# Moving the MAX8 over the candidate sums ahead of the first one-hots in a product-key expert kernel

## The reference, cut to what matters

```
xn  = batchnorm(x) * gamma + beta
sim = einsum(q(xn), keys)                  # per token, 8 heads, 2 sides, 32 keys
s, i = top_k(sim, 8)                       # (sx, ix) and (sy, iy)
all_scores = sx[..., :, None] + sy[..., None, :]
scores, pk = top_k(all_scores, 8)          # of 64 sums per head
idx = (ix * 32 + iy)[pk]                   # one of 1024 experts
o   = gelu(x . key_in[idx]) * softmax(scores)
out = layernorm(x + sum over heads and k of o * key_out[idx])
```

## Time and profile before

| | |
|---|---|
| time, median of 3 runs | 588.12 us (588.06 to 588.79) |
| the profiled execution's own time | 586.68 us |
| its span in the trace | 584.9 us |
| DVE busy | 490.1 us, 84% of the span |
| TensorE matmul, ACT, POOL busy | 308.8, 263.6 and 288.7 us |

### The profile page before, as it was taken

How to read it: one execution, slowest core, us unless ns; L and a number is a source line. 1 busy time by engine, 2 the same in 40 slices (tenths; PEclk the granted TensorE clock), 3 DMA queues, 4 the chain that set the end, 5 groups by cost and what they waited for, 6 DMA issues and landing times.

```text
span 584.9 us, 14423 instructions
## 1 busy us (share of the span) xinstructions
PE 308.8 (53%) x5105; PEld 198.8 (34%) x5105; DVE 490.1 (84%) x2777; ACT 263.6 (45%) x416; POOL 288.7 (49%) x307
## 2 busy tenths in 40 slices
PE   5687575124142818272836465446545563456845
PEld 3233462013122316132722252226223521442544
DVE  2557896899899989899898989998989898984834
ACT  4877523314233642574166325812671455225721
POOL 1143411361623689278917881867198639840000
PEclk9898765665555758695769595958586877597988
DMA  8800000000023003200410050005000500140051
GB/s 232 239 0 2 0 2 1 1 0 3 2 56 92 1 3 90 68 10 2 119 47 2 2 145 21 1 2 145 21 1 13 135 20 1 30 117 1 16 150 36
DMA packets 49848, 26.69 MB, mean 46 GB/s; under 512 B 3056, under 2 KB 49008, under 8 KB 49776
## 3 DMA queue, kind: packets, MB, share of 16 engines
q1 hardware_dynamic: 49200, 25.70, 16.9%
q10 hardware_dynamic: 576, 0.07, 0.1%
HBM read 6.88 MB, written 2.10 MB: 15 GB/s over the span
## 4 chain that ended last, share of the span: by engine, by line
DVE 34%; issue 24%; POOL 23%; PE 9%; ACT 6%; SPq 2%; DMA 1%; POOLq 0%; DVEq 0%; ACTq 0%
DVE picked L743 7%; DVE arena L693 6%; POOL arena L331 5%; POOL code L317 5%; POOL iyf L311 4%; PE psum L845 4%; DVE arena L691 3%; DVE words L729 3%; DVE arena L586 2%; SPq L216 2%; PE psum L957 2%; DVE stage L641 2%; DVE arena L681 1%; PE psum L947 1%; DVE arena L805 1%
## 5 line engine op out<-in xcount | busy, mean ns | idle before, releaser
L933 PE MATMUL psum<-arena 64*64 64x64 f16 x4096 | 53.5, 218 | 132.6 <-DVE arena L693 100.1
L933 PEld LDWEIGHTS psum<-arena 64*64 64x64 f16 x4096 | 49.9, 131 | 146.7 <-issue 102.1
L331 POOL TENSOR_TENSOR arena<-arena 128x512 f32<-128x512 f32 x48 | 87.7, 1857 | 0.0
L710 DVE FIND_INDEX8 idx<-vals,sims 128x8 uint32<-128x32 f32 x512 | 82.7, 184 | 0.0
L957 PE MATMUL psum<-ko,arena 128*128 128x128 f32 x512 | 65.3, 293 | 22.0 <-POOL arena L331 13.2
L957 PEld LDWEIGHTS psum<-ko,arena 128*128 128x128 f32 x512 | 63.8, 208 | 30.8 <-POOL arena L331 21.0
L947 PE MATMUL psum<-x1T,trn 128*128 128x512 f32 x128 | 64.3, 643 | 18.8 <-ACT arena L484 18.8
L304 POOL CAST lists<-wk 128x128 f16<-128x128 f32 x16 | 4.6, 290 | 110.1 <-DVE wk L760 110.1
L911 PE MATMUL psum<-msim,xn 128*128 128x512 f32 x64 | 56.0, 1028 | 4.6 <-ACT xn L436 4.6
L703 DVE MAX8 vals<-sims 128x8 f32<-128x32 f32 x512 | 49.0, 175 | 3.4 <-ACT sims L444 3.4
L693 DVE TENSOR_TENSOR arena<-arena,listsT 128x2048 f16<-128x2048 f16 x32 | 47.3, 1479 | 0.0
(11 more groups left out here) (109 smaller groups left out, 690.0 us busy)
## 6 DMA issues: line engine op xcount, KB each, us to landing
arena<-arena SPq DMA_DIRECT2D x64, 128.0 KB
arena<-stage SPq DMA_DIRECT2D x64, 128.0 KB
stage<-in_L_attn_x_dram SPq DMA_DIRECT2D x8, 256.0 KB, 4.4
x<-in_L_attn_x_dram SPq DMA_DIRECT2D x4, 512.0 KB, 7.1
out_dram<-nat SPq DMA_DIRECT2D x8, 256.0 KB, 2.2
nat<-in_L_ffn_key_in_dram SPq DMA_DIRECT2D x4, 128.0 KB, 4.2
ko<-in_L_ffn_key_out_dram SPq DMA_DIRECT2D x4, 128.0 KB, 4.3
nat<-in_L_ffn_keys_dram SPq DMA_DIRECT2D x2, 128.0 KB, 3.5
```

Of the source, the lines that this page charges most:

```text
L331: pool.tensor_tensor(by_token, pt[:, jh].rearrange("p (c n) -> p n c", c=4), by_token, ALU.mult).then_inc(s["a_done"], 1)
L710: last = dve.max_index(idx[:, p, t * H + h, :], vals[:, p, t * H + h, :], sims[:, t, r, :])
L933: last = pe.matmul(psum[64 * e:64 * e + 64, at:at + 2 * NK], hotx[rows, par, two, :, e].rearrange("p b i -> p (b i)"), hotw[rows, par, par ...
```

## The change

The 16 instructions over the candidate sums go from behind the first `hot_y` and `hot_x` to a place directly behind the index search. Nothing is added or removed.

```
--- before.py
+++ after.py
@@ -709,13 +709,13 @@
                         last = dve.max_index(idx[:, p, t * H + h, :], vals[:, p, t * H + h, :], sims[:, t, r, :])
                     last.then_inc(s["idx_done"], 1)
-                if hot_before:
-                    hot_y(m - 1, 0)
-                    hot_x(m - 1, hot_par, 0)
                 wait(dve, "cand_done", m + 1)
                 for r in range(RH):
                     last = dve.max(top[:, r, :], cand[:, r, :])
                 last.then_inc(s["top_done"], 1)
+                if hot_before:
+                    hot_y(m - 1, 0)
+                    hot_x(m - 1, hot_par, 0)
                 if hot_before:
                     hot_w(m - 1, hot_par, 0)
                     hot_y(m - 1, 1)
```

## The result

The changed kernel takes 591.89 us in the median of 4 runs (590.86 to 593.37), the kernel before 588.09 (587.94 to 588.79). The ratio is 1.0064 with a 95% interval of 1.0041 to 1.0087: slower, by an amount inside the predicted range and 0.4 us from the predicted 592.3. The profiled execution takes 590.86 us with a span of 589.1; the prediction said 590.8 and 589.1. That agreement is an accident, as the rows show.

The account below looks back on a forecast made before the run. DVE, busy 490.1 of 584.9 us, was taken to bound the kernel. Step 2 -1.05, steps 4, 6, 8, 12, 14 +4.45, L318's holds +0.63, odd steps +0.12: +4.15 on 588.12 gives 592.3 us, range 589.4 to 593.8.

Parts of the forecast that it names:

- who holds the port: DVE against POOL at the one-hots: a POOL start some 0.06 us ahead wins; the loser waits for the whole row.
- T: Start of the first DVE instruction behind a step's index search: the first one-hot before the change, the moved MAX8 after.
- turns: Form of a step where POOL slips one instruction between each two of DVE: 24.01 us in step 3, 29.30 in step 10.
- all nine steps: Steps 1 to 4, 6, 8, 10, 12, 14: L318, 0.13 us ahead of the one-hot, should start turns in each.
- locked: Form of a step where POOL waits until the row of one-hots is through: 25.06 us in step 2, 28.41 in step 4.
- 9 x 0.07: L318 holds up the first one-hot by 0.07 us (bounds 0 and 0.14) in each of nine steps: +0.63 us.
- Rival 1: L318 does not start the turns, L319 is locked out behind six one-hots, all nine steps locked: 589.45 us, chance 0.11.
- Odd steps: Steps 5 to 15: `dif` freed, L317 still locked out, 2.42 us gap before L729 stays; +0.02 each, +0.12 us for six.
- Rival 3: Nothing measurable: timed runs already take turns in most even steps and lose only small terms, +0.8, 588.9 us; chance 0.08.

Follow-up runs that it names:

- after_third: The changed kernel, unedited, in a third profile on a third chip: 593.14 us, ratio 1.0095.
- after_again: The changed kernel, unedited, in a new profile: 591.89 us, ratio 1.0045.
- before_again: The kernel before the change, unedited, in a new profile: 588.66 us (one run).
- before_third: The kernel before the change, unedited, in a third profile on the chip of after_third: 587.86 us (one run).
- mixed: Changed kernel with one unused extra MAX8 in steps 1 to 3, two in odd steps from 5, and the old order in even steps from 4: 579.92 us.
- weigh_later: Changed kernel with one unused extra MAX8 per step (two in odd steps from 5), even steps' four `weigh` waiting for the last one-hot: 572.15 us.
- pad1_all: Changed kernel with one more MAX8, its result unused, ahead of the first one-hot in steps 1 to 15: 592.37 us, ratio 1.0054.
- pad2_odd: Changed kernel with two more MAX8, results unused, ahead of the first one-hot in odd steps from 5 only: 583.72 us, ratio 0.9898.

## Why the prediction was right in its time and half right in its reasons

- **Right: what bounds.** From step 1 to step 15 the kernel is as long as DVE's steps together. The stretches ahead of and behind them differ between profiles by up to 3 us, and the prediction had no term for them.
- **Right: who holds the port.** Starts decide, and a loser on POOL waits for the whole row of one-hots (7.12 to 7.18 us for six in the profiles of the changed kernel), not for one instruction. The Trainium skill, page "SBUF — State Buffer", section "Who interferes with whom", says that whoever issues first gets the shared pair for the whole instruction while the other fully blocks. Once DVE has won, these rows do not agree that the wait ends with one instruction.
- **The step that failed: "POOL, with a MAX8 beside it, runs as in step 0: L311 at T + 0.15, L318 at T + 1.17", and from it "It should hold the one-hot up and start the turns, in all nine steps and not in three".** I took one profile's distance for a constant. It is 0.14 to 0.17 in some executions and 0.19 to 0.23 in others, in both kernels. Added to that, the one-hot started 1.28 and not 1.30 behind T. Of 0.13 us margin 0.04 was left in the first profile of the changed kernel, and all nine steps were locked. Where the distance is 0.15 the step is right as written (after_third: L318 at 1.17, one-hot at 1.29).
- **The term 9 x 0.07 for L318 holding the one-hot up** measured 0.07 to 0.11 in after_third (24.08 to 24.09 for 24.01; 29.37 to 29.41 for 29.30), where there are turns.
- **Rival 1 happened in the first profile of the changed kernel and in after_again, with its price wrong.** I had given it 0.11 and had it cost nothing against the locked form of before, "locked out behind six" with L319 the first to wait. It is L318, so one POOL instruction more is left to run behind the lock: 25.31 against 25.06 us, 28.70 against 28.41. Nine times 0.25 to 0.30 and five times about 0.05 make 2.7 from before_again to the first profile of after (387.73 - 385.03). To after_again, on the same chip as before_again, it is 2.85 (387.88 - 385.03). That is 0.48% of 588, and agrees with the ratio measured there, 1.0045 (1.0025 to 1.0064).
- **Odd steps: right in form**, L317 7.13 us long for 7.1, 2.41 idle for 2.4, and +0.03 to +0.06 each for the predicted 0.02. The MAX8 started 0.10 us later behind the last search than before in the first profile of after, outside my bound of 0.07, and 0.02 later in after_third.
- **The sum.** From the first profile of before to after_third the steps grew by 4.38 (388.18 - 383.80), predicted 4.15. Between the two first profiles they grew by 3.93 through the other mechanism: steps 1 and 3 lost their turns (+1.3 each) and 0.25 to 0.30 came on step 2 and on the even ones, while step 10 gained 0.6. The span grew by 4.18 for the predicted 4.15, but 0.43 of it came ahead of step 1 and -0.18 behind step 14, where the prediction has nothing. Two routes to nearly one number: the time could not tell them apart, and the hit is luck. Nor do the steps explain all of the third pair. From before_third to after_third they grew by 3.57, 0.6%, where the timed runs give 0.95% (0.62 to 1.28); between the two profiles another 2.24 us lie ahead of step 1 and 0.47 behind step 14. What makes these stretches differ stays open.
- **Rival 3** guessed rightly that another execution need not have the form of the first profile. No trace shows which form the timed runs had; before_again is locked in all steps, not in turns, and before_third takes turns in one even step from 4 more (6 and 10).

## What to carry to other kernels

Where two engines hold each other up, read who starts first at each meeting and by how much, and do so in more than one profile: here the starts moved by 0.06 us between executions, so a margin under 0.1 us is not a margin. Placing work by 0.08 to 0.16 us of padding, with each step in the form that suits it, gave 1.7%; padding in every step and POOL's long instructions moved out of the one-hots gave 3.0% together. And when a moved instruction opens a window, count what the waiting engine still has to run when the window shuts, because that is what stands behind the lock.

## What the runs showed of the hardware that I had not expected

- Turns or lock is a matter of some 0.06 us. Over all profiles POOL won with starts 0.055 us ahead and more, and lost with 0.063 and less, so between these two it can go either way; a TENSOR_TENSOR of fp16 on DVE that starts unhindered shuts POOL out for its whole row, one that POOL has held up once takes turns until POOL has nothing more. How long it is held up does not matter: in steps 1 to 3 of mixed and weigh_later POOL starts 0.17 to 0.19 us ahead and delays the second one-hot by only some 0.02 us (1.14 to 1.15 behind the first, for 1.12 to 1.13 in locked steps), and the turns come all the same.
- There are two kinds of execution. The last search of step 1's row, in after_third and in after:

```profile
126.69 0.18 DVE L710 FIND_INDEX8 idx<-vals,sims 128x8 uint32<-128x32 f32 x1
```

```profile
125.27 0.25 DVE L710 FIND_INDEX8 idx<-vals,sims 128x8 uint32<-128x32 f32 x1
```

  The searches start every 0.16 us in both, but in the second kind the last of them ends some 0.06 us later behind its start, and POOL, which waits for the end, comes that much later against DVE's next start. All four profiles from one chip (after_again, before_again, pad1_all, pad2_odd) are of the second kind, all six from two others of the first, and both kernels are among each, so it may belong to the chip or to the moment. What causes it stays open.
- Small DVE instructions on 16-bit data (TENSOR_SCALAR, 128 x 128 uint16) wait beside a running GpSimd instruction as well: 1.36 to 1.53 us in weigh_later for 0.22 in after_third.
